# An adaptive-layer-norm block with holographic attention and a mixture of experts: adding DMAs for low weight halves, a sum moved into the inverse transform, and an epsilon moved to ScalarE

## The chip, the cores and the metric

The kernel runs on one core of a Trainium2 chip. The metric is the device time of one execution in microseconds (us); lower is better.

## The reference, cut to what matters

x has 4x1024 tokens of 256 features. The weights, a bias for each projection and the modulation vectors come in as inputs.

```python
def unit_projection(x):
    f = fft(x); f = f / (abs(f) + 1e-8); return ifft(f).real
h = layernorm(x) * (1 + ca) + sa
query, keys, values = (unit_projection(h @ W.T + b) for W, b in ((Wq, bq), (Wk, bk), (Wv, bv)))
s = cumsum(ifft(fft(keys) * fft(values)).real, axis=1)          # binding, running sum over tokens
x = x + ga * ifft(fft(s) * conj(fft(query))).real               # unbinding
h = layernorm(x) * (1 + cb) + sb
weights, sel = top_k(h @ gate_w, 2); weights = softmax(weights)
x = x + gb * sum(weights[k] * expert(sel[k], h))                # 8 experts, 256 -> 2x512 (swiglu) -> 256
```

## The kernel before, in words

The kernel has three stages. The attention stage goes over NBLK = 8 blocks of 512 tokens, t = 0 to 7. The routing stage sorts the (token, expert) pairs into tiles. The expert stage runs 39 tiles of up to 256 rows through the two expert products on TensorE. Each engine has its own program, written out by hand in one fixed order, and waits on semaphores; there is no scheduler. Iteration t of an engine's loop works on block t and also on neighbours of it.

In the attention stage the blocks are spectra with frequencies on the 128 partitions and tokens along the row. TensorE transposes the normalised rows (`project`, line 501), ScalarE scales them out of PSUM (`spectra`, line 894), and TensorE forms the six spectra (real and imaginary part of key, value, query) of block t+1 in `transform`, line 530. ScalarE copies these (line 909) and squares them (line 916) in `evacuate`. VectorE adds the squares (`magnitudes`, line 1305), ScalarE takes the roots (`roots`, line 935), and VectorE's `bind` adds epsilon to the value magnitudes (line 1248), multiplies the magnitudes, takes one reciprocal (line 1258), scales the spectra, multiplies key and value (line 1273) and runs the two running sums (lines 1282 and 1285). GpSimd multiplies the sums by the query's four combinations (line 1660; in block 7 VectorE takes half of them, line 1294), and in even blocks scales the inverse matrix (line 1669). VectorE's `unbind` adds two products to the real part (line 1299) and subtracts two for the imaginary part (line 1300). TensorE copies the Nyquist row (line 609), ScalarE writes it into the imaginary part (line 1033), and TensorE's `inverse` makes the rows of the block by two products for each of four token groups (lines 625 and 629). In block 7 it adds x by a third product with the identity (line 621).

The residual of a block is copied by ScalarE (`residual`, line 955), which stands inside `evacuate` two blocks on, behind the squares of the key. GpSimd then adds x to it by an accumulating DMA (line 1655). SP stores the sum (line 398), and VectorE takes its moments (line 1222, with the same line for the moments of a later block of x) behind the running sums of the next block. Then come `top2` on the gate scores of an earlier block, the Nyquist product (line 1241), `unbind`, `magnitudes` of the next block and the second layer norm (lines 1397 and 1402). ScalarE copies that to a high fp16 half (`split_rows`, line 966) and GpSimd forms the low half (`low_rows`, line 1646); SP stores both (line 422).

Beside this the expert weights are split into a high and a low fp16 half. They come in 24 chunks of 128x1024 fp32 numbers through a pair of staging buffers; SP loads chunk n (line 368) when the low half of chunk n-2 is out. ScalarE makes the high half by a scaled copy (`split_weights`, line 974), two chunks at the end of each iteration, behind `split_rows` and ahead of the next `evacuate`. The low half of the chunks 0 to 17 is made by TensorE in four pieces an iteration (`low_piece`, lines 589 and 590: 64 times the chunk less the high half, into a rotating PSUM bank), which ScalarE copies to fp16 (line 981). `psum_plan` gives the order in which four PSUM banks rotate among spectra, Nyquist columns, pieces, gate scores and Nyquist rows. ScalarE's standard deviations (lines 872 and 930) stand ahead of the pieces 1 and 2 and of line 1033; line 880 (four normalised row groups) follows line 1033, and then piece 3, the roots and the spectra.

Of the kernel before, what the change touches and what calls it, by code (L numbers as in the profile page):

```python
# [27 lines left out]
P = 128  # L28
# [6 lines left out]
BLK = 512  # L35
# [46 lines left out]
def psum_plan():  # L82

    items = []
    for t in range(-1, NBLK + 2):
        if t + 1 < NBLK:
            items += [("z", t + 1, i) for i in range(6)]
        if t == -1:
            items += [("ny", 0, 0), ("lo", 0, 0)]
        elif t == 0:  # L90
            items += [("pre", 0, 0), ("ny", 1, 0), ("row", 0, 0), *(("lo", 1, i) for i in range(4))]
            continue
        elif t < NBLK:
# [9 lines left out]
        if t < NBLK:  # L103
            items.append(("lo", t + 1, 2))
        if 0 <= t < NBLK:
            items.append(("row", t, 0))
        if t < NBLK:
            items.append(("lo", t + 1, 3))
    return {item: n for n, item in enumerate(items)}, items


def adaln_moe_kernel(nc, x, wqkv, bqkv, gate_w, w1, b1, w2, b2, c_t, wmod, dft, idft, ident, tri, iota, ramp, out):
# [11 lines left out]
    with ExitStack() as ctx:  # L124
# [73 lines left out]
        eps_col = carve(1)  # L198

# [115 lines left out]
        w_in = sems("w_in", 4)  # L315
        iota_in, gb_in = sem("iota_in"), sem("gb_in")
        w_lo = sems("w_lo", 2)
        lo_mm, w_hi, gate_split, h2_hi, h2_lo, hid_hi, y_mid = (sem(n) for n in (
# [39 lines left out]
        def load_weights(sp, n):  # L358

            if n in (18, 19):  # L360
                sp.wait_ge(prod_ready, 2 * NBLK)
            elif n >= 20:
                sp.wait_ge(w_lo[n % 2], 2 * (n // 2 - 1))
            elif n >= 2:
                sp.wait_ge(w_lo[n % 2], 2 * (n // 2))
            at = (n if n < W1_CHUNKS else W2_ORDER[n - W1_CHUNKS]) * WCH
            src = (w1 if n < W1_CHUNKS else w2)[:, at:at + WCH]
            sp.dma_start(staged(n), src).then_inc(w_in[stage_of(n)], 16)

# [79 lines left out]
        def _(pe):  # L449
# [162 lines left out]
            def inverse(t):  # L612
# [5 lines left out]
                for j in range(TPB):  # L618
                    cols = ps[:, OUT + j // 2, (j % 2) * D:(j % 2 + 1) * D]
                    if t == LAST:  # L620
                        pe.matmul(cols, ident_sb[:], x_sb[:, t % XS, j, :], start=True, stop=False)
                    if j == 0:
                        pe.wait_ge(g_ready, 2 * t + 1)
                        pe.wait_ge(ga_ready, t // 2 + 1)
                    pe.matmul(cols, prod[:, 0, RE, j * P:(j + 1) * P], idft_ga[:, RE, :], start=(t < LAST), stop=False)  # L625
                    if j == 0:
                        pe.wait_ge(g_ready, 2 * t + 2)
                        pe.wait_ge(row_ready, t + 1)
                    mm = pe.matmul(cols, prod[:, 0, IM, j * P:(j + 1) * P], idft_ga[:, IM, :], start=False, stop=True)  # L629
                    if t == LAST and j == 1:  # L630
                        mm.then_inc(l_idft, 1)
# [62 lines left out]
            for t in range(-1, NBLK):  # L694
# [20 lines left out]
                elif t + 1 < NBLK:  # L715
                    project(t + 1)
                    transform(t + 1)
                    low_piece(t + 1, 0)
# [5 lines left out]
                low_piece(t + 1, 1)  # L724
# [4 lines left out]
                low_piece(t + 1, 2)  # L729
                if t >= 0:  # L730
                    nyquist_row(t)
                low_piece(t + 1, 3)
# [104 lines left out]
        def _(act):  # L837
# [60 lines left out]
            def evacuate(t):  # L898
# [7 lines left out]
                for c in range(3):  # L906
# [6 lines left out]
                    if c == 2 and t >= 2:  # L913
                        low_piece(t, 0)
# [17 lines left out]
            def roots(t):  # L932
                act.wait_ge(mag_ready, t + 1)
                act.wait_ge(ny_out, 2 * t + 2)
                nc.scalar.activation(mag[:, t % 2], mag[:, t % 2], ACT.Sqrt).then_inc(root_ready, 1)

# [31 lines left out]
            def split_weights(n):  # L968
# [5 lines left out]
                nc.scalar.activation(parts_of(n)[HI], staged(n), ACT.Copy, scale=SW).then_inc(w_hi, 1)  # L974

            def low_piece(t, i):
# [3 lines left out]
                act.wait_ge(lo_mm, 4 * t + i + 1)  # L980
# [3 lines left out]
            def low_weights(t):  # L984

                act.wait_ge(g_ready, 2 * NBLK)
                for i in range(4):
                    act.wait_ge(lo_mm, 4 * t + i + 1)
# [40 lines left out]
            def nyquist_row(t):  # L1029

                act.wait_ge(row_mm, t + 1)
                act.wait_ge(g_ready, 2 * (t + 1))
# [15 lines left out]
            for t in range(-1, NBLK):  # L1048
# [32 lines left out]
                low_piece(t + 1, 1)  # L1081
                if t >= 2:
                    gate(t - 2)
                low_piece(t + 1, 2)
# [4 lines left out]
                low_piece(t + 1, 3)  # L1089
# [85 lines left out]
        def _(dve):  # L1175
            V = nc.vector
            V.memset(warm, 0.0).then_inc(warm_set, 1)
            V.memset(eps_col, EPS_LN)
            V.memset(ny_run[:, 0:1], 0.0)
# [109 lines left out]
            def unbind(t):  # L1289
# [9 lines left out]
                V.tensor_tensor(prod[:, 0, RE, 0:BLK], prod[:, 0, RE, 0:BLK], prod[:, 1, IM, 0:BLK], ALU.add).then_inc(g_ready, 1)  # L1299
# [342 lines left out]
        def _(pool):  # L1642
# [131 lines left out]
```

## Time and profile before

| | us |
|---|---|
| median of 3 runs | 595.83 |
| lowest and highest of them | 595.48, 599.93 |
| the profiled execution | 594.5 |
| its span in the profile | 592.5 |
| TensorE busy | 548.7 |
| VectorE busy | 478.2 |
| ScalarE busy | 294.4 |
| GpSimd busy | 294.8 |

The profile is of one execution. Its span runs from the first to the last recorded instruction; the execution's own time has 2 us around that. PE is TensorE's products, PEld its weight loads, DVE is VectorE, ACT ScalarE, POOL GpSimd, SPq the DMA issues of SP. A busy time is summed over the engine's instructions. An fp32 product shows as two instructions.

### The profile page before, as it was taken

Reading aid. Unit: us, or ns where it says so; the run is one execution under the profiler, and the core shown is the slowest. Engines: PE = TensorE matmul, PEld = TensorE weight load, DVE = VectorE, ACT = ScalarE, POOL = GpSimd, SP = SyncE. Lnnn points to the kernel's source line nnn. Section 1 sums busy time; section 2 is a strip of 40 time slices with the busy share of each in tenths; the row PEclk is TensorE's granted clock in tenths of the full one; section 3 lists DMA queues with packets and bytes.
Section 4 is the critical chain, followed back from the end, with each engine's and each line's share of the span. In section 5 each row is a group of like instructions: output and inputs, shape, how many; then the busy total and the mean of one; then the engine's idle time right before and its main releaser. Section 6 shows DMA issues by size and latency. Waiting matters only on the chain.

```text
span 592.5 us, 13011 instructions
## 1 busy us (share of the span) xinstructions
PE 548.7 (93%) x3955; PEld 407.6 (69%) x3956; DVE 478.2 (81%) x1059; ACT 294.4 (50%) x497; POOL 294.8 (50%) x197
## 2 busy tenths in 40 slices
PE   8998999999999995667999999999999999999992
PEld 6545565555646552526588888888888888888771
DVE  1288979999999989999488888888888888888762
ACT  4776678879696863641533333333333333333330
POOL 0004033432423242000548888888888888887532
PEclk9998989999897977866999999999999999999998
DMA  8333633653745437723567787777777777765722
GB/s 310 121 99 122 184 97 109 191 160 107 212 107 153 125 97 246 289 42 70 144 118 137 143 134 136 131 138 129 139 134 135 141 129 133 130 98 86 113 38 28
DMA packets 81571, 79.32 MB, mean 134 GB/s; under 512 B 44596, under 2 KB 71348, under 8 KB 81272
## 3 DMA queue, kind: packets, MB, share of 16 engines
q0 software_dynamic: 16912, 31.74, 30.2%
q1 hardware_dynamic: 63320, 46.15, 27.5%
q10 hardware_dynamic: 1296, 0.87, 0.5%
q8 instruction: 25, 0.41, 0.3%
q14 instruction: 18, 0.15, 0.1%
HBM read 44.06 MB, written 22.23 MB: 112 GB/s over the span
## 4 chain that ended last, share of the span: by engine, by line
PE 73%; DVE 17%; ACT 3%; issue 3%; DMA 2%; POOL 1%; POOLq 0%; DVEq 0%; ACTq 0%
PE ps L778 31%; PE ps L799 15%; PE ps L530 11%; PE ps L589 4%; DVE region L1258 2%; PE ps L543 2%; PE ps L629 2%; PE ps L625 1%; DMA region<-in_dft 1%; PE ps L600 1%; PE ps L461 1%; PE ps L590 1%; DVE region L1273 1%; DVE region L1380 1%; DMA out_rows<-w_stage,region 1%
## 5 line engine op out<-in xcount | busy, mean ns | idle before, releaser
L778 PE MATMUL ps<-region,w_sb 128*128 128x256 f16 (+1 forms) x1872 | 200.4, 264 | 1.9 <-ACT region L1026 1.3
L778 PEld LDWEIGHTS ps<-region,w_sb 128*128 x1872 | 172.6, 98 | 24.9 <-issue 3.2
L1690 POOL DMA_INDIRECT out_rows<-w_stage,region x71 | 135.7, 1912 | 49.6 <-issue 20.0
L1680 POOL DMA_INDIRECT region<-h_scratch,region x71 | 95.9, 1351 | 71.5 <-DVE region L1539 45.0
L1571 DVE TENSOR_SCALAR region<-ps,region 128x256 f32<-128x256 f32 (+1 forms) x156 | 64.3, 454 | 55.3 <-PE ps L778 53.8
L799 PE MATMUL ps<-region 128*128 x852 | 99.5, 273 | 3.5 <-DVE region L1585 3.3
L1130 ACT ACTIVATE region<-ps,region 128x256 f32<-128x256 f32 (+1 forms) x156 | 62.2, 451 | 79.2 <-PE ps L778 74.2
L1142 ACT ACTIVATE region<-region 128x1024 f16<-128x1024 f32 (+1 forms) x39 | 38.2, 981 | 109.4 <-DVE region L1579 106.8
L799 PEld LDWEIGHTS ps<-region 128*128 128x128 f16 x852 | 82.6, 98 | 14.4 <-issue 4.3
L530 PE MATMUL ps<-region 128*128 128x512 f32 x192 | 84.2, 595 | 3.2 <-ACT region L894 3.2
L1660 POOL TENSOR_TENSOR region<-region 128x512 f32<-128x512 f32 x30 | 37.3, 1270 | 96.2 <-DVE region L1285 96.2
L530 PEld LDWEIGHTS ps<-region 128*128 128x128 f32 x192 | 35.9, 190 | 46.9 <-issue 44.7
L589 PE MATMUL ps<-w_stage,ident_sw 128*128 128x512 f32 x72 | 47.0, 740 | 1.2 <-ACT region L974 1.2
L1579 DVE SCALAR_TENSOR_TENSOR region<-region 128x1024 f32<-128x1024 f32 (+1 forms) x39 | 44.0, 1129 | 1.4
L1585 DVE SCALAR_TENSOR_TENSOR region<-region 128x1024 f16<-128x1024 f32 (+1 forms) x39 | 43.8, 1124 | 1.1 <-ACT region L1142 1.1
L1646 POOL TENSOR_TENSOR region<-region 128x1024 f16<-128x1024 f32 x6 | 12.8, 2133 | 52.9 <-ACT region L966 45.4
L909 ACT ACTIVATE region<-ps,region 128x512 f32<-128x512 f32 x48 | 31.8, 683 | 11.1 <-PE ps L530 10.8
L1604 DVE SCALAR_TENSOR_TENSOR w_stage<-w_stage,region 128x256 f32<-128x256 f32 x71 | 31.3, 478 | 0.8
L1598 DVE SCALAR_TENSOR_TENSOR w_stage<-ps,region 128x256 f32<-128x256 f32 x71 | 26.8, 415 | 2.5 <-PE ps L799 2.4
L1258 DVE RECIPROCAL region<-region 128x516 f32<-128x516 f32 x8 | 27.0, 3378 | 0.3
L981 ACT ACTIVATE w_sb<-ps 128x512 f16<-128x512 f32 x32 | 18.7, 589 | 14.6 <-PE ps L590 14.4
L916 ACT ACTIVATE region<-region 128x1024 f32<-128x1024 f32 x24 | 25.3, 1055 | 0.5
(229 smaller groups left out, 699.2 us busy)
## 6 DMA issues: line engine op xcount, KB each, us to landing
w_stage<-in_w SPq DMA_DIRECT2D x20, 512.0 KB, 3.8
region<-in_x SPq DMA_DIRECT2D x8, 512.0 KB, 7.5
out_rows<-region SPq DMA_DIRECT2D x8, 512.0 KB, 3.0
h_scratch<-gb_bc SPq DMA_DIRECT2D x4, 1024.0 KB, 6.7
h_scratch<-region SPq DMA_DIRECT2D x8, 512.0 KB, 3.2
region<-region POOLq DMA_DIRECT2D x7, 512.0 KB, 4.6
region<-in_ramp SPq DMA_DIRECT2D x1, 2064.0 KB, 10.6
region<-in_w SPq DMA_DIRECT2D x4, 512.0 KB, 6.0
```

Source lines behind the costliest of these rows:

```text
L530: mm = pe.matmul(rot(("z", t, i)), w_spec[:, c, k, r * P:(r + 1) * P], h_t[:, k, :], start=(k == 0), stop=(k == KD - 1))
L589: pe.matmul(rot(("lo", t, i)), ident_sw[:], staged(n)[:, at:at + BLK], start=True, stop=False)
L778: mm = pe.matmul(ps[:, GV + 2 * half + a, (f % 2) * MT:(f % 2) * MT + wide], w, xg_t[:, s, xa * KD + k, 0:wide], start=(n == 0), stop=(n = ...
L799: mm = pe.matmul(ps[:, YB + s, u * D:(u + 1) * D], hid[:, s, xa, k, u * P:(u + 1) * P], w, start=(n == 0), stop=(n == 3 * KF - 1))
L1130: ins = nc.scalar.activation(gs[:, 2 * half + f, 0:wide], ps[:, 4 + 2 * half, f * MT:f * MT + wide], ACT.Gelu_apprx_sigmoid, scale=1.0 / S ...
L1142: nc.scalar.activation(hid[:, s, HI, :, 0:wide], vv[:, s, :, 0:wide], ACT.Copy, scale=SH / SUP).then_inc(hid_hi, 1)
L1258: V.reciprocal(rec, rec).then_inc(rec_ready, 1)
L1571: ins = V.tensor_scalar(vv[:, s, 2 * half + f, 0:wide], ps[:, 5 + 2 * half, f * MT:f * MT + wide], b1_t[:, bass.ds(e, 1), 1, 2 * half + f] ...
L1579: V.scalar_tensor_tensor(out=vv[:, s, :, 0:wide], in0=vv[:, s, :, 0:wide], scalar=(1.0 - LIMIT) * SUP, in1=gs[:, :, 0:wide], op0=ALU.max, ...
L1585: V.scalar_tensor_tensor(out=hid[:, s, LO, :, 0:wide], in0=vv[:, s, :, 0:wide], scalar=SH / SUP, in1=hid[:, s, HI, :, 0:wide], op0=ALU.mul ...
L1680: G.indirect_dma_start(out=xg_rows[:, t % XG, u, :], out_offset=None, in_=h_scratch, in_offset=bass.IndirectOffsetOnAxis(ap=gather_idx[:, ...
L1690: G.indirect_dma_start(out=out, out_offset=bass.IndirectOffsetOnAxis(ap=scatter_idx[:, at:at + 1], axis=0), in_=y_sb[:, t % 2, u, :], in_o ...
```

## The change

Chunks 4 to 15 no longer pass through TensorE. Behind the high half ScalarE overwrites the staging buffer with the high half times -1/64. GpSimd then loads the same chunk again from memory with an adding DMA into the staging buffer, which leaves the remainder, and ScalarE copies that times 64 as the low half (`low_chunk`). The pieces of chunks 0 to 3, 16 and 17 stay. The real sum of the unbinding (line 1299) goes: TensorE adds a third product per token group in `inverse`, with the same matrix. The epsilon of the value magnitudes (line 1248) moves to ScalarE, behind the roots. The new semaphores are w_neg, w_acc and unit_set; g_ready counts one instead of two for each block.

```diff
@@ psum_plan @@
-        elif t < NBLK:
+        elif t == NBLK - 1:
             items.append(("lo", t + 1, 0))
-            if t + 1 < NBLK:
-                items.append(("ny", t + 1, 0))
-        if t < NBLK:
+        elif t + 1 < NBLK:
+            items.append(("ny", t + 1, 0))
+        if t == -1 or t == NBLK - 1:
             items.append(("lo", t + 1, 1))
...
+        def summed(n):
+            return 4 <= n < 2 * NBLK
...
@@ pe inverse @@
                     if j == 0:
-                        pe.wait_ge(g_ready, 2 * t + 1)
+                        pe.wait_ge(x1_ready, 2 * t + 1)
                         pe.wait_ge(ga_ready, t // 2 + 1)
                     pe.matmul(cols, prod[:, 0, RE, j * P:(j + 1) * P], idft_ga[:, RE, :], start=(t < LAST), stop=False)
+                    if j == 0 and t < LAST:
+                        pe.wait_ge(x1_ready, 2 * t + 2)
+                    if j == 0 and t == LAST:
+                        pe.wait_ge(x1_own, 1)
+                    pe.matmul(cols, prod[:, 1, IM, j * P:(j + 1) * P], idft_ga[:, RE, :], start=False, stop=False)
                     if j == 0:
-                        pe.wait_ge(g_ready, 2 * t + 2)
+                        pe.wait_ge(g_ready, t + 1)
                         pe.wait_ge(row_ready, t + 1)
@@ pe loop (the same for the pieces 0, 2 and 3) @@
-                low_piece(t + 1, 1)
+                if t in (-1, LAST):
+                    low_piece(t + 1, 1)
@@ act evacuate @@
-                    if c == 2 and t >= 2:
-                        low_piece(t, 0)
@@ act roots @@
                 nc.scalar.activation(mag[:, t % 2], mag[:, t % 2], ACT.Sqrt).then_inc(root_ready, 1)
+                act.wait_ge(root_ready, t + 1)
+                nc.scalar.activation(mag[:, t % 2, VAL, :], mag[:, t % 2, VAL, :], ACT.Identity,
+                                     bias=eps_unit).then_inc(eps_ready, 1)
@@ act split_weights @@
                 nc.scalar.activation(parts_of(n)[HI], staged(n), ACT.Copy, scale=SW).then_inc(w_hi, 1)
+                if summed(n):
+                    act.wait_ge(w_hi, n + 1)
+                    nc.scalar.activation(staged(n), parts_of(n)[HI], ACT.Copy, scale=-1.0 / SW).then_inc(w_neg, 1)
+
+            def low_chunk(n):
+                act.wait_ge(w_acc[n % 2], 16 * (n // 2 - 1))
+                nc.scalar.activation(parts_of(n)[LO], staged(n), ACT.Copy, scale=SW).then_inc(w_lo[n % 2], 2)
@@ act loop (the same for piece 2 and chunk 2 * t + 3, behind the gate; piece 3 has no such part) @@
-                low_piece(t + 1, 1)
+                if t in (-1, LAST):
+                    low_piece(t + 1, 1)
+                else:
+                    low_chunk(2 * t + 2)
@@ dve bind, unbind @@
-                dve.wait_ge(root_ready, t + 1)
-                V.tensor_scalar(mag[:, s, VAL, :], mag[:, s, VAL, :], EPS_UNIT, None, ALU.add).then_inc(eps_ready, 1)
                 dve.wait_ge(eps_ready, t + 1)
...
-                V.tensor_tensor(prod[:, 0, RE, 0:BLK], prod[:, 0, RE, 0:BLK], prod[:, 1, IM, 0:BLK], ALU.add).then_inc(g_ready, 1)
@@ gpsimd @@
+            def add_weights(n):
+                pool.wait_ge(w_neg, n - 3)
+                G.dma_start(staged(n), source_of(n), accum_op=ALU.add).then_inc(w_acc[n % 2], 16)
+
             for t in range(NBLK):
                 s, b = t % 2, t // 2
                 if t >= 2:
                     pool.wait_ge(all_ready, t + 1)
                     low_rows(t - 2)
+                    for n in (2 * t + 2, 2 * t + 3):
+                        if summed(n):
+                            add_weights(n)
                 if t >= 1:
                     pool.wait_ge(x2_ready, t)
                     G.dma_start(x2, x_sb[:, (t - 1) % XS], accum_op=ALU.add).then_inc(x2_sum, 16)
+                if t == 1:
+                    for n in (4, 5):
+                        add_weights(n)
```

## Rows read from the trace of the kernel before

**Rows 1.** The page: busy time of each engine
```profile
PE 548.7 (93%) x3955; PEld 407.6 (69%) x3956; DVE 478.2 (81%) x1059; ACT 294.4 (50%) x497; POOL 294.8 (50%) x197
```

**Rows 2.** Chain of waits, core 0: start us, us, what
```profile
88.42 0.79 ACT region L894
...
138.86 0.45 PE ps L501 x4
...
139.34 0.79 ACT region L894
...
160.34 0.86 PE ps L589 x2
...
161.20 0.22 PE ps L590
...
164.59 0.43 PE ps L629 x2
...
165.50 0.79 ACT region L894
...
192.93 0.79 ACT region L894
...
218.94 0.71 DVE region L1250
```

**Rows 3.** Timeline of ScalarE: start us, us, line, idle before and who ended it
```profile
69.69 1.06 ACT L974 ACTIVATE w_sb<-w_stage 128x1024 f16<-128x1024 f32 x1 [3.43 <-DMA w_stage<-in_w]
...
141.63 1.99 ACT L974 ACTIVATE w_sb<-w_stage 128x1024 f16<-128x1024 f32 x2
...
143.52 1.25 ACT L909 ACTIVATE region<-ps,region 128x512 f32<-128x512 f32 x2
...
145.77 1.01 ACT L955 ACTIVATE region<-ps 128x1024 f32<-128x1024 f32 x1
...
157.28 0.28 ACT L930 ACTIVATE region<-region 128x4 f32<-128x4 f32 x1
...
161.03 0.59 ACT L1033 ACTIVATE region<-ps 1x512 f32<-1x512 f32 x1 [0.50 <-DVE region L1300]
...
163.97 1.48 ACT L935 ACTIVATE region<-region 128x1548 f32<-128x1548 f32 x1
```

**Rows 4.** Timeline of VectorE in block 4
```profile
139.59 0.42 DVE L1248 TENSOR_SCALAR region<-region 128x516 f32<-128x516 f32 x1
...
153.54 1.38 DVE L1222 BATCH_NORM_STATS2 region<-region 128x6 f32<-128x256 f32 x4
...
158.78 1.11 DVE L1299 TENSOR_TENSOR region<-region 128x512 f32<-128x512 f32 x1
...
159.81 1.13 DVE L1300 TENSOR_TENSOR region<-region 128x512 f32<-128x512 f32 x1
...
165.76 0.42 DVE L1248 TENSOR_SCALAR region<-region 128x516 f32<-128x516 f32 x1
```

**Rows 5.** Timeline of GpSimd in block 4
```profile
141.87 2.13 POOL L1646 TENSOR_TENSOR region<-region 128x1024 f16<-128x1024 f32 x1 [8.43 <-ACT region L966]
...
147.07 0.89 POOL L1655 DMA_DIRECT2D region<-region  x1 [3.07 <-ACT region L955]
```

**Rows 6.** Timeline of SP's queue in block 4
```profile
151.60 0.39 SPq L398 DMA_DIRECT2D out_rows<-region  x1
```

**Rows 7.** Stretches of DMA work: us, engines' busy us, clock, DMA share, GB/s
```profile
148.30:151.10 2.80, 2.80 (x8) 1.17 (x7) 2.77 (x3) 1.77 (x3) 0.00 (x0) 1.00 0.98 187
```

**Rows 8.** DMA issues of the page: KB each, median us from issue to landing
```profile
w_stage<-in_w SPq DMA_DIRECT2D x20, 512.0 KB, 3.8
...
region<-region POOLq DMA_DIRECT2D x7, 512.0 KB, 4.6
```

**Rows 9.** Stretches of TensorE: length, busy us (instructions), granted clock, DMA share, GB/s
```profile
183.00:184.00 1.00, 1.00 (x23) 0.50 0.37 122
...
189.00:190.00 1.00, 1.00 (x6) 1.00 0.00 0
```

More of the change, by code:

```diff
@@ L102, in psum_plan @@
             items.append(("gate", t - 2, 0))
-        if t < NBLK:
+        if t == -1 or t == NBLK - 1:
             items.append(("lo", t + 1, 2))
@@ L106, in psum_plan @@
             items.append(("row", t, 0))
-        if t < NBLK:
+        if t == -1 or t == NBLK - 1:
             items.append(("lo", t + 1, 3))
@@ L198, in adaln_moe_kernel @@
         eps_col = carve(1)
+        eps_unit = carve(1)
         wmod_sb = z_flat[:, 6 * NB:6 * NB + 6 * BLK].rearrange("p (k n) -> p k n", k=KD)
@@ L315, in adaln_moe_kernel @@
         w_in = sems("w_in", 4)
+        unit_set = sem("unit_set")
         iota_in, gb_in = sem("iota_in"), sem("gb_in")
         w_lo = sems("w_lo", 2)
+        w_neg, w_acc = sem("w_neg"), sems("w_acc", 2)
         lo_mm, w_hi, gate_split, h2_hi, h2_lo, hid_hi, y_mid = (sem(n) for n in (
@@ L368, in load_weights, with pieces_to, source_of @@
             sp.dma_start(staged(n), src).then_inc(w_in[stage_of(n)], 16)
+        def summed(n):
+            return 4 <= n < 2 * NBLK
+        def pieces_to(t, i):
+            return 4 * (t if t < 2 else t - NBLK + 2) + i + 1
+        def source_of(n):
+            at = (n if n < W1_CHUNKS else W2_ORDER[n - W1_CHUNKS]) * WCH
+            return (w1 if n < W1_CHUNKS else w2)[:, at:at + WCH]
         def parts_of(n):
@@ L717, in _ @@
                     transform(t + 1)
-                    low_piece(t + 1, 0)
                     nyquist_cols(t + 1)
@@ L728, in _ @@
                     gate(t - 2)
-                low_piece(t + 1, 2)
+                if t in (-1, LAST):
+                    low_piece(t + 1, 2)
                 if t >= 0:
                     nyquist_row(t)
-                low_piece(t + 1, 3)
+                if t in (-1, LAST):
+                    low_piece(t + 1, 3)
                 if t >= 0:
@@ L934, in roots @@
                 act.wait_ge(ny_out, 2 * t + 2)
+                if t == 0:
+                    act.wait_ge(unit_set, 1)
                 nc.scalar.activation(mag[:, t % 2], mag[:, t % 2], ACT.Sqrt).then_inc(root_ready, 1)
+                act.wait_ge(root_ready, t + 1)
+                nc.scalar.activation(mag[:, t % 2, VAL, :], mag[:, t % 2, VAL, :], ACT.Identity,
+                                     bias=eps_unit).then_inc(eps_ready, 1)
             def gate_rows(t):
@@ L979, in low_piece @@
                     act.wait_ge(tp_done, KD * NBLK)
-                act.wait_ge(lo_mm, 4 * t + i + 1)
+                act.wait_ge(lo_mm, pieces_to(t, i))
                 nc.scalar.activation(parts_of(2 * t + i // 2)[LO][:, (i % 2) * BLK:(i % 2 + 1) * BLK],
@@ L984, in low_weights @@
             def low_weights(t):
-                act.wait_ge(g_ready, 2 * NBLK)
+                act.wait_ge(idft_done, NBLK)
                 for i in range(4):
-                    act.wait_ge(lo_mm, 4 * t + i + 1)
+                    act.wait_ge(lo_mm, pieces_to(t, i))
                     nc.scalar.activation(parts_of(2 * t + i // 2)[LO][:, (i % 2) * BLK:(i % 2 + 1) * BLK],
@@ L1031, in nyquist_row @@
                 act.wait_ge(row_mm, t + 1)
-                act.wait_ge(g_ready, 2 * (t + 1))
+                act.wait_ge(g_ready, t + 1)
                 nc.scalar.activation(prod[0:1, 0, IM, 0:BLK], rot(("row", t, 0))[0:1, :], ACT.Copy).then_inc(row_ready, 1)
@@ L1080, in _ @@
                     std2(t - 1)
-                low_piece(t + 1, 1)
+                if t in (-1, LAST):
+                    low_piece(t + 1, 1)
+                else:
+                    low_chunk(2 * t + 2)
                 if t >= 2:
                     gate(t - 2)
-                low_piece(t + 1, 2)
+                if t in (-1, LAST):
+                    low_piece(t + 1, 2)
+                else:
+                    low_chunk(2 * t + 3)
                 if t >= 1:
@@ L1088, in _ @@
                     normal_rows(t + 2)
-                low_piece(t + 1, 3)
+                if t in (-1, LAST):
+                    low_piece(t + 1, 3)
                 if 1 <= t < NBLK - 1:
@@ L1178, in _ @@
             V.memset(eps_col, EPS_LN)
+            V.memset(eps_unit, EPS_UNIT).then_inc(unit_set, 1)
             V.memset(ny_run[:, 0:1], 0.0)
```

## The prediction

> **What bounds the kernel now.** I read the page's busy shares first: TensorE is busy 93% of the span, VectorE 81%, ScalarE and GpSimd 50% [rows 1]. A share does not say what a change in the attention part is worth, so the chain of waits came next. Up to 250 us it passes through one hand-over per block: the transposes of line 501 release ScalarE's spectra (line 894), and those release the transforms. Call the start of line 894 X. X was at 88.42, 139.34, 165.50 and 192.93 us [rows 2]: two blocks (t=2 and 3) took 50.92 us, t=4 26.16, t=5 27.43. After 290 us the expert part runs on TensorE alone, and nothing of the change reaches it.
>
> Block 4 in the timelines shows two full engines. VectorE goes from line 1248 at 139.59 to the next one at 165.76, 26.17 us, with no gap above 0.2 us [rows 4]. TensorE's transposes end where line 894 starts [rows 2]. Work taken off one of them alone would give nothing. This change takes work off both and gives it to ScalarE, GpSimd and the DMA queue, so the question is what these now hold up.
>
> **The parts, in block 4.** I count from X and from g, the end of line 1300 (159.81+1.13 = 160.94 [rows 4]).
>
> VectorE loses line 1248 (0.46 with its hand-over) and line 1299 (159.81-158.78 = 1.03; 0.6 in odd blocks, where GpSimd does not work beside it) [rows 4]. On its own it would need 24.7 us for block 4; without GpSimd beside it 24.4, which I take as its bound.
>
> TensorE loses four low pieces in each of t=1 to 6: 0.86+0.22 = 1.08 each [rows 2], 4.3 a block. It gains four products in the inverse transform, each a pair of instructions of 0.43 together [rows 2], 1.7 a block. Some 22.5 us are left, so its sum no longer binds. But the pieces stood ahead of g and most new products stand behind it. From g to the next X it was 165.50-160.94 = 4.56, with seven products behind the Nyquist row. Now ten are behind it; two of the twelve can run once GpSimd's products are there and g isn't. So g to X becomes 4.56+3x0.43 = 5.86.
>
> ScalarE loses four copies of line 981 a block, and gains two negatives, two low copies (both like line 974, 0.95 each back to back) and the epsilon (at most like line 909, 0.65). The low copies stand between line 930 (ends 157.56) and line 1033 (161.03) [rows 3], where ScalarE had only two low pieces: 157.5+2x0.95+0.15 = 159.55, against g at about 159.9. They cost nothing with top2 ahead of g (t=3 to 6), 0.5 us without (t=2); if that cover goes, they cost up to their 1.9. The epsilon ends at g+0.1+0.5+2.0+1.48+0.7 = g+4.8 (line 1033, four rows of line 880, roots), and VectorE comes for it at 165.76-160.94 = g+4.82: nothing, with no cover left, and up to 0.65 a block if it is late.
>
> The negatives are dear. Line 974 took 143.52-141.63 = 1.89 for two [rows 3]. A negative waits for its own high half, so the four take 2x(1.09+0.95) = 4.08: 2.2 more (bounds 1.9 if they pipeline, 2.4 if all drain). Line 955, the copy of the residual, stands behind them. It ended at 146.78, X+7.4; it will end at X+9.6.
>
> GpSimd waits for line 955 and adds x by an accumulating transfer (issued 147.07 [rows 5]); SP sees it landed at 151.60 [rows 6], 4.85 behind line 955. VectorE wanted it at 153.54, for line 1222 [rows 4]: 1.9 us of cover. Now it comes at X+9.6+4.85 = X+14.45. VectorE would be at line 1222 13.5 us after line 1250, which is at g+4.86 with X at g+5.86, so at X+12.5. The cover is gone and 1.95 us of wait take its place.
>
> The loop that sets the period then is: X to the sum 14.45; the sum to g, 5.24 for lines 1222 to 1299 and 0.7 for line 1300, or 1.05 beside GpSimd's line 1669 in even blocks, so 5.95 or 6.3; g to X 5.86. That is 26.25 or 26.6 us. Before, the same loop was 12.3+7.4+4.56 = 24.2 and lay under VectorE's 26.2.
>
> **The queue.** The adding loads go on GpSimd's DMA queue ahead of the x sum. Let δ be the delay they bring. The x transfer of 512 KB kept the 16 DMA engines busy from 148.30 to 151.10, share 0.98 [rows 7]; I take 2.7 us for an add too, the nearest row. The first can be issued when line 1646 ends, X+4.7 [rows 5], and move from X+6.0; the second moves to 11.4, where the x sum would begin at 11.2: δ 0.2. SP's store of h2 falls in the same stretch and can push all by 1.15: δ 1.35. I take 0.75, midway. Bounds: 0 if an add moves fast; 3.5 if each of the three holds the queue for 3.8, the time in which a plain load lands [rows 8].
>
> The Trainium skill ("DMA: Bandwidth & Descriptors", Anatomy of one DMA, SWDGE path) gives 2.0 us plus bytes over 436 GB/s, an estimate from that page of 3.2 us for 512 KB with 1.2 of moving. The trace disagrees for an accumulating transfer: 4.6 to landing, 2.8 of moving at 187 GB/s [rows 7, 8]. By the page δ would be 0 and the sum 3.8 us lower.
>
> **The clock.** TensorE's granted clock was 0.50 (1.2 GHz) at 183 us, after the light work of lines 543 and 564 and gaps between it, and 1.00 (2.4 GHz) again at 189 after further low pieces had run [rows 9]. The low pieces took the slow time on them and the inverse always ran fast. Without them TensorE has only light work from about X+12 to X+19.7, so I expect the inverse to start at the low clock and be the work that brings it back. If it stays low for R from the time that GpSimd's products are there, the 5.65 us of inverse and first transposes end R/2 later than 5.75, against 6.6 at full clock. R near 4 (the low stretches with low pieces in them lasted from under 4 to about 7 us) gives 1.15, R 2 nothing, R 7 gives 2.65. I take 1.0 for each X of t=1 to 5, 5 us; bounds 0 and 13. Blocks 0 and 7 keep their low pieces, and in t=6 no spectra follow.
>
> **The sum.** Blocks 0 and 1: VectorE's parts fall, but chunk 5 came only at 69.69 [rows 3], its negative delays the copies behind it, and the low copies push line 1033 by 1.5: the X at 88.42 comes 0.6 earlier. t=2 and 3: 2x26.2 against 50.92, +1.5. t=4: 26.6 against 26.16, +0.4. t=5: 26.2 against 27.43, whose pieces ran slowly, -1.2. t=6, to line 1250 at 218.94 [rows 2]: 14.45+6.3+4.85 = 25.6 against 26.0, -0.4. t=7: four more products, 1.7, partly beside ScalarE's lines 966 and 974, less line 1299: +0.7. Together +0.4, with 5δ = 3.75 and the clock's 5: +9.2. The profiled execution took 594.5 us (span 592.5), so 603.7. It lay 1.3 below the median of the runs, so I give 605 for that.
>
> **Rivals.** (1) VectorE stays the bound; faster. For it: it is the fullest engine and over 1 us leaves each block. It decides if the x sum lands over 1.95+δ earlier than worked out, and TensorE follows. Then t=3 to 6 take 24.4 each where they took about 105.1 together: -7.5; t=2 -1.5, blocks 0 and 1 -1: 584.5, on the median 586. Against it: the negatives stand ahead of line 955 in program order, and the cover was only 1.9. Chance 0.13. (2) The loop binds, but nothing queues and the clock is back in time: +0.4, 595, on the median 596; with one of the two at half price up to 600. For it: neither is seen in the trace before. Chance 0.34. (3) The adds are slow: the GpSimd queue decides from δ 2 on. At δ 3.5, 5x3.5 for 3.75 is +13.8 on my sum: 619. Against: the transfer like it took 2.8. Chance 0.08. My forecast, loop and queue and clock: 0.45, own range 600 to 612.
>
> 1% (6 us) is what a measurement tells from no change. Faster by more: 0.13 from (1). Same: 0.35, from (2) and the lower edge of mine. Slower: 0.52. The range 590 to 613 leaves out most of (1) and of (3).
>
> **What would show it.** VectorE waits 2 to 4 us at the first line 1222 behind the scans in t=2 to 6, released by the accumulating transfer. Line 955 starts some 8.6 us behind the first line 894, not 6.4. Two adds stand between lines 1646 and 1655. From g to the next X 5.9 to 7.5 us, with the first products of the inverse at granted clock 0.50. Blocks of 27 to 29 us. If VectorE doesn't wait, (1) holds and the forecast is wrong; if inverse products start at 1.00, the clock's term is; if the wait is over 5 us, it is (3).

## The result, and the profile after

The kernel after took 615.07 us (median of 3 runs, 612.92 to 616.55) where the kernel before took 595.83. The ratio is 1.029, 95% interval 1.024 to 1.034: slower. The sign and the main cause were as forecast; 615 lies above the range (590 to 613), and 10 us above the 605. The two medians alone would give 1.032; the ratio is nearer to that of the means, and one of the three executions of the kernel before took 599.93. The profiled execution took 616.55 us with a span of 614.5, against 594.5 and 592.5.

The page's busy times and queues:

```profile
PE 546.8 (89%) x3947; PEld 417.1 (68%) x3948; DVE 472.9 (77%) x1044; ACT 309.2 (50%) x505; POOL 303.9 (49%) x209
...
PE 65%; DVE 14%; DMA 10%; ACT 5%; issue 4%; POOL 1%; POOLq 0%; SPq 0%; DVEq 0%; ACTq 0%
...
w_stage<-in_w POOLq DMA_DIRECT2D x12, 512.0 KB, 7.6
...
region<-region POOLq DMA_DIRECT2D x7, 512.0 KB, 6.9
```

Both full engines of before are a little less busy than in [rows 1] and yet the span is 22 us longer, so the loss is not work added to them. DMA is now 10% of the chain that ended last, 2% before. An adding load takes 7.6 us from issue to landing (median), and the x sum 6.9, 4.6 before [rows 8].

The chain of waits up to the start of block 4's loop (start us, us, what; line 517 is line 501 of before, 546 is 530, 917 is 894, 932 is 909, 981 is 955, 1264 is 1222; 641, 646 and 650 are the three inverse products, the second of them new; 1003 is the negative copy, 1008 the low copy, 1283 is 1241, 1290 is 1250, 1339 is 1300, 625 is 609 and 1067 is 1033):

```profile
92.61 0.79 ACT region L917
...
121.76 0.79 ACT region L917
...
143.78 1.01 PE ps L625 x4
144.79 0.85 PE ps L641 x2
...
148.21 0.60 PE ps L646 x2
148.81 0.43 PE ps L650 x2
...
151.84 0.45 PE ps L517 x4
152.31 0.79 ACT region L917
```

Against [rows 2] the spectra of block 2 begin 4.2 us late (92.61 for 88.42) and the hand-over then takes 29 to 31 us a block, not 25 to 27. The rest of block 4 is in the timelines of ScalarE, GpSimd, SP and VectorE (start us, us, line; in brackets the idle time before and who ended it):

```profile
158.68 1.25 ACT L932 ACTIVATE region<-ps,region 128x512 f32<-128x512 f32 x2
...
160.92 1.01 ACT L981 ACTIVATE region<-ps 128x1024 f32<-128x1024 f32 x1
...
154.85 2.56 POOL L1685 TENSOR_TENSOR region<-region 128x1024 f16<-128x1024 f32 x1 [14.56 <-ACT region L992]
...
157.36 0.86 POOL L1690 DMA_DIRECT2D w_stage<-in_w  x1
159.07 0.86 POOL L1690 DMA_DIRECT2D w_stage<-in_w  x1 [0.86 <-ACT w_stage L1003]
162.22 0.86 POOL L1702 DMA_DIRECT2D region<-region  x1 [2.29 <-ACT region L981]
...
169.16 0.39 SPq L414 DMA_DIRECT2D out_rows<-region  x1
...
155.45 2.51 DVE L1303 TENSOR_TENSOR region<-region 128x516 f32<-128x516 f32 x1
...
169.17 1.41 DVE L1264 BATCH_NORM_STATS2 region<-region 128x6 f32<-128x256 f32 x4 [3.93 <-DMA region<-region]
...
173.54 0.14 DVE L1283 TENSOR_TENSOR region<-ps,region 128x4 f32<-128x4 f32 x1
...
173.89 0.69 DVE L1339 TENSOR_TENSOR region<-region 128x512 f32<-128x512 f32 x1
...
179.80 0.70 DVE L1290 SCALAR_TENSOR_TENSOR region<-region 128x516 f32<-128x516 f32 x1 [0.32 <-ACT region L960]
```

VectorE had no gap above 0.2 us in [rows 4]; now it waits 3.93 us for the x sum. That is the transfer whose cover the prediction saw vanish. Over the five blocks with adds (t=2 to 6) these waits are 3.9, 4.1, 3.9, 4.3 and 5.0.

The inverse transform of that block, in TensorE's timeline, and the stretches of its light work and its products (length, busy us and instructions of the five engines, granted clock, DMA share, GB/s):

```profile
173.74 1.01 PE L625 MATMUL ps<-ident_sb,region 128*1 128x128 f32 x4 [4.50 <-DVE region L1283]
174.55 1.06 PE L641 MATMUL ps<-region 128*128 128x256 f32 x2
...
178.81 0.76 PE L650 MATMUL ps<-region 128*128 128x256 f32 x2
179.41 0.59 PE L641 MATMUL ps<-region 128*128 128x256 f32 x2
```
```profile
158.50:169.00 10.50, 9.31 (x72) 6.05 (x71) 6.67 (x7) 9.82 (x15) 5.34 (x5) 1.00 0.97 196
174.50:178.00 3.50, 3.50 (x11) 2.75 (x10) 3.50 (x8) 3.50 (x7) 0.00 (x0) 0.50 1.03 312
```

TensorE stands idle for 4.50 us until VectorE's line 1283 and then runs its first five products at a granted clock of 0.50 (1.2 GHz): 0.85 from one pair to the next, 0.43 behind. Before, the pairs of this transform took 0.43 [rows 2]. The clock had fallen at 168.95, behind light work (lines 559 to 592) and 0.3 us before this idle time began, and it was back at about 179.15. The DMA engines are busy for 0.97 of 10.5 us while two adds, the x sum and SP's store pass.

Block 4's loop against the prediction's terms (X the start of line 917, g the end of line 1339):

| step | predicted | measured |
|---|---|---|
| X to the end of line 981 | 9.6 | 161.93-152.31 = 9.62 |
| to line 1264, the x sum landed | 4.85+0.75 = 5.6 | 169.17-161.93 = 7.24 |
| to g | 6.3 | 174.58-169.17 = 5.41 |
| g to the next X | 5.86+1.0 = 6.86 | 182.65-174.58 = 8.07 |
| whole | 28.35 | 30.34 |

### The profile page after: what moved, and what is told of

The parts are those of the page before. It is cut to its first block, busy times and chain, and to the rows that moved or that the text cites. A ratio compares the mean times of both kernels' runs of the same rounds, so it can differ in the third digit from the quotient of the medians.

```text
span 614.5 us, 12988 instructions
## 1 busy us (share of the span) xinstructions
PE 546.8 (89%) x3947; PEld 417.1 (68%) x3948; DVE 472.9 (77%) x1044; ACT 309.2 (50%) x505; POOL 303.9 (49%) x209
## 4 chain that ended last, share of the span: by engine, by line
PE 65%; DVE 14%; DMA 10%; ACT 5%; issue 4%; POOL 1%; POOLq 0%; SPq 0%; DVEq 0%; ACTq 0%
PE ps L801 30%; PE ps L822 14%; DMA region<-region 7%; PE ps L546 6%; DMA w_stage<-in_w 3%; PE ps L650 2%; PE ps L641 2%; PE ps L646 2%; DVE region L1264 2%; PE ps L469 1%; ACT region L932 1%; DVE region L1298 1%; PE ps L616 1%; PE ps L477 1%; ACT region L981 1%
## 5 line engine op out<-in xcount | busy, mean ns | idle before, releaser
L1264 DVE BATCH_NORM_STATS2 region<-region 128x6 f32<-128x256 f32 x60 | 20.8, 411 | 22.6 <-DMA region<-region 21.1
L932 ACT ACTIVATE region<-ps,region 128x512 f32<-128x512 f32 x48 | 30.6, 679 | 5.6 <-PE ps L546 5.6
L625 PE MATMUL ps<-ident_sb,region 128*1 128x128 f32 x32 | 7.7, 389 | 22.9 <-DVE region L1283 22.9
```

The source lines that it names most:

```text
L932: nc.scalar.activation(z[:, t % 2, c, r, 0:BLK], rot(("z", t, 2 * c + r)), ACT.Identity, bias=bias_f[:, 3 * r + c:3 * r + c + 1]).then_inc ...
```

## The experiments

Ratios are to the kernel before, timed again beside each group of runs (medians 594.2, 594.8 and 594.3), with 95% intervals. Medians of one kernel scatter by 2 to 3 us, so intervals between hand-overs (X to X) are compared beside them. The 1.029 of the change rests on three executions on either side, so half a percent between it and a run below is not resolved. "Waits" are VectorE's for the x sum in t=2 to 6.

**The pieces back on TensorE; the moved sum and epsilon stay.** From the kernel before:

```diff
-V.tensor_tensor(prod[:, 0, RE, 0:BLK], prod[:, 0, RE, 0:BLK], prod[:, 1, IM, 0:BLK], ALU.add)
+pe.matmul(cols, prod[:, 1, IM, j * P:(j + 1) * P], idft_ga[:, RE, :], start=False, stop=False)
-V.tensor_scalar(mag[:, s, VAL, :], mag[:, s, VAL, :], EPS_UNIT, None, ALU.add)
+nc.scalar.activation(mag[:, t % 2, VAL, :], mag[:, t % 2, VAL, :], ACT.Identity, bias=eps_unit)
```

> The adding loads, the negatives and the low copies are undone: TensorE makes all low halves by pieces as before; the sum in the inverse and the epsilon on ScalarE stay. Theory (loop: the negatives and adds delay the x sum, and the inverse runs at the low clock for want of pieces ahead of it): the wait of VectorE for the x sum goes to 0, the inverse runs at granted clock 1.00, but TensorE, full before, has 1.7 us more a block: 603 to 607 us. Rival A (the third product alone is the loss, whatever stands ahead of it): about the time of the changed kernel, 612 to 616. Rival B (all of the loss is the adds): 594 to 597.

600.98 us, 1.0105 (1.0067 to 1.0143). No waits, intervals 24.6 to 29.1, inverse pairs at 0.43. That is less than the 603 to 607 expected. Undoing the adding loads and what serves them takes away 1.85% (1.0292/1.0105), nearly two thirds of the loss, and leaves about 1%. The parts need not add up so in another order, as the next run shows.

**The real sum back on VectorE, in the kernel after.**

```diff
+V.tensor_tensor(prod[:, 0, RE, 0:BLK], prod[:, 0, RE, 0:BLK], prod[:, 1, IM, 0:BLK], ALU.add)
-pe.matmul(cols, prod[:, 1, IM, j * P:(j + 1) * P], idft_ga[:, RE, :], start=False, stop=False)
```

> Only the sum of the real part goes back to VectorE (eight products a block in the inverse); adds and epsilon stay as changed. Theory: the wait for the x sum stays at 4 to 5 us a block, g comes 0.7 later and the inverse saves four products at a clock that is low for half of them, 1.7 to 2.5 us: 608 to 612 us. Rival A (the third product is the loss): 596 to 600. Rival B (all of the loss is the adds): 613 to 617.

612.28 us, 1.0290 (1.0243 to 1.0338): the ratio shows no difference from the change. The waits stay at 4.0 to 5.1. The profiled execution shows a small one: intervals of 28.6 to 29.8 in t=2 to 5 in place of 29.1 to 30.6, and g to X of 5.1 to 6.4 us in place of 7.7 to 8.2, of which the later g takes back more than half. So while the x sum binds, returning the sum is worth under 1 us a block of 30, and the medians do not tell it from nothing.

**The x sum ahead of the two adds in GpSimd's queue.**

```diff
-low_rows(t - 2); add_weights(2 * t + 2); add_weights(2 * t + 3); G.dma_start(x2, ...)
+low_rows(t - 2); G.dma_start(x2, ...); add_weights(2 * t + 2); add_weights(2 * t + 3)
```

> The changed kernel with GpSimd's x sum issued ahead of the two adding loads of the block. Theory (the x sum queues behind the adds, 7.2 us from line 981 to landing where it was 4.85): it lands 4.9 us after line 981 again, VectorE's wait falls by 2.4 in t=2 to 6, up to 12 us; the low copies come to wait for the later adds and give back about 1 us a block: 603 to 609 us. Rival C (the x sum is late only because ScalarE's negatives stand ahead of it, the queue has no part): the landing stays near 7 us behind line 981 and the time at 613 to 616.

611.66 us, 1.0282 (1.0232 to 1.0333), where 603 to 609 was expected. The x sum landed 5.2 us behind the copy, not 7.2, and the waits fell to 1.6 to 3.1. Yet intervals stayed near 30.6: the adds came later, and ScalarE's low copy, line 1008, stands ahead of the row copy of line 1067 that the inverse needs. ScalarE's timeline:

```profile
170.27 1.04 ACT L1008 ACTIVATE w_sb<-w_stage 128x1024 f16<-128x1024 f32 x1
...
172.76 1.06 ACT L1008 ACTIVATE w_sb<-w_stage 128x1024 f16<-128x1024 f32 x1 [1.36 <-DMA w_stage<-in_w]
173.72 0.57 ACT L1067 ACTIVATE region<-ps 1x512 f32<-1x512 f32 x1
```

So the queue does delay the x sum, but the order only chooses which of three transfers is late.

**Twelve idle products on TensorE ahead of line 625, t=1 to 6.** They add work that nothing uses.

```diff
+for _ in range(12):
+    pe.matmul(rot(("row", t, 0)), ident_h[:], w1_sb[:, HI, 0:BLK], start=True, stop=True)
 nyquist_row(t)
```

> The changed kernel with twelve idle fp16 products of 512 columns into the bank of the Nyquist row, in t=1 to 6, ahead of the row's transposes. They compute nothing that is used. Theory (the inverse starts at the low clock because only light work stands ahead): the inverse's products run at 1.00, 0.43 a pair, g to the next X falls from 8.1 to about 5.4 us, five times: 600 to 604 us. Rival D (the slow pairs are slow for another reason, such as operands or a busy memory port): pairs stay at 0.85 and the time at 613 to 617.

611.48 us, 1.0274 (1.0231 to 1.0316). Its chain of waits:

```profile
166.32 5.14 PE ps L755 x12
171.46 0.44 PE ps L625 x4
171.90 0.43 PE ps L641 x2
172.33 0.43 PE ps L646 x2
```

All pairs but one run in 0.43, and g to X falls from 8.07 to 6.26 us. The granted clock was 0.50 in 166 to 170, under the idle products, and 1.00 from 172: they took the slow time on them. So the slow pairs come from the want of such products ahead of the inverse, and not from its operands or the DMA beside it. The 600 to 604 expected was missed: the span is 7.5 us shorter, but the ratio gains only 0.2%. The profiled executions exaggerate, since 616.55 was the highest of the change's three and 608.83 the lowest of this kernel's four; the ratio may hide some, since all four (up to 612.3) lie below all three of the change (from 612.92). What the mechanism is worth in the whole stays between the two.

**Epsilon back on VectorE, in the kernel after.**

```diff
-nc.scalar.activation(mag[:, t % 2, VAL, :], mag[:, t % 2, VAL, :], ACT.Identity, bias=eps_unit)
+V.tensor_scalar(mag[:, s, VAL, :], mag[:, s, VAL, :], EPS_UNIT, None, ALU.add)
```

> Only the epsilon goes back to VectorE. Theory: VectorE comes 0.3 us early for it in the changed kernel but waits 4 us for the x sum later in the same block, so the move costs and saves nothing while the loop binds: 611 to 615 us, X to X the same within 0.3 us. Rival: the epsilon behind the roots delays bind and with it the loop by 0.3 to 0.7 a block: 608 to 611.

617.43 us, 1.0367 (1.0330 to 1.0404), above the 611 to 615 expected. Nothing comes back. The intervals of t=2 to 5 are the change's within 0.35 us (29.5, 30.6, 30.2, 30.4), as expected; the profiled execution is 2.2 us longer because the spectra of block 2 begin at 94.72 and not at 92.61. That start is unsteady: the run with the x sum first and the one with late copies, whose programs are the same up to there, have 90.59 and 94.78. So the extra is not shown to be epsilon's. The 0.32 us for which VectorE waits at line 1290 is not a loss.

**Eight of the twelve products ahead of line 625.** Those that need no g, in a loop of their own.

```diff
+if t >= 1:
+    inverse_head(t)    # RE and the third product, all four j; t=1 to 7
 nyquist_row(t)
 if t in (-1, LAST):
     low_piece(t + 1, 3)
```

> The changed kernel with the eight products of the real part (two a token group) issued ahead of the Nyquist row's transposes in t=1 to 7; the four imaginary products stay behind. Same products, other order. Theory (the new products cost because program order puts them between g and the next X, at the low clock, while TensorE idles some 4 us ahead): g to the next X falls from 8.1 to 4 to 5 us, in five blocks 15 to 20 us: 594 to 600 us. Rival (the loop passes over the x sum and the adds alone, and X would be held by something else): under 5 us gained, 608 to 612.

615.88 us, 1.0347 (1.0303 to 1.0390), far above both the 594 to 600 expected and the rival's 608 to 612. Odd blocks fell to 25.2, 27.7 and 27.6, even ones took 30.8 and 30.6. In even blocks GpSimd scales the inverse matrix behind its products, and TensorE's program order then holds up the row transposes:

```profile
168.84 1.20 POOL region L1755 x2
...
170.18 3.62 PE ps L638 x8
173.80 1.73 PE ps L650 x8
175.53 0.45 PE ps L625 x4
...
176.00 0.02 ACT region L1103
```

The row copy (line 1103 there) came at 176.00, 3.6 behind g, and with it the roots and epsilon, for which VectorE then waited 3.47 us. The first four of the eight products ran at a granted clock of 0.50, 0.9 us each for 0.43, so the low clock makes about half of the 3.6. An early start is worth 2 to 3 us where the matrix is ready, and where it isn't it gains nothing or costs up to 1.7 (30.8 for 29.15 in t=2). By the X of block 6 this run was 5.0 us ahead (208.24 for 213.26) and it lost them again from there on: block 7 has the same order, with x's four products besides.

**The x sum first, and the high and negative copies of chunks 6 to 15 behind the residual copy.** The order of GpSimd's queue is that of the third run; ScalarE's calls at the end of each iteration go for these chunks.

```diff
 residual(t - 2)
+split_weights(2 * t)
+split_weights(2 * t + 1)
```

> The changed kernel with the x sum issued ahead of the adds, and with ScalarE's high halves and negatives of the chunks 6 to 15 moved behind the residual's copy (line 981). Theory: line 981 ends at X+7.0 rather than 9.6 minus nothing else, actually about X+5.6 as the high halves go too; the x sum lands at X+11; VectorE's wait goes to 0 to 0.5; but ScalarE's four copies now stand ahead of the standard deviations and low copies, so some 2 us come back: dX 27 to 28 where it was 30.4, 600 to 605 us. Rival (the adds' own landing holds the low copies and so line 1067, whatever the order): dX stays above 29.5, 609 to 614.

603.18 us, 1.0122 (1.0083 to 1.0162): the largest step of all. ScalarE's and VectorE's timelines:

```profile
147.66 1.45 ACT L917 ACTIVATE region<-ps,region 128x512 f32<-128x512 f32 x2 [1.89 <-PE ps L517]
...
153.97 1.01 ACT L983 ACTIVATE region<-ps 128x1024 f32<-128x1024 f32 x1
154.88 1.05 ACT L1002 ACTIVATE w_sb<-w_stage 128x1024 f16<-128x1024 f32 x1
...
160.79 1.38 DVE L1266 BATCH_NORM_STATS2 region<-region 128x6 f32<-128x256 f32 x4
```

The residual copy (line 983) ends 7.3 us behind X, as before the change, and VectorE finds the sum there: one wait of 0.24 us in t=2, none behind it. Intervals are 26.2 to 28.2. Against the run with the queue order alone (1.0282) only the copies moved, so these four copies ahead of the residual were 1.6% of the time, nearly 10 us. The loop theory holds. Late copies with the old queue order were not run.

**The same, with the first of the three products ahead of line 625.**

> e7's order together with the four first products (prod 0 RE) ahead of the Nyquist row's transposes, the four third products right behind them, then the four imaginary ones. Theory: both halves of the loop shrink, dX 25 to 26.5 (then ScalarE or VectorE with 24.4 binds): 586 to 594 us, at or below the kernel before. Rival (TensorE's low clock at these products keeps them slow): dX 27 to 28, 597 to 603.

611.63 us, 1.0270 (1.0235 to 1.0306). It gives the gain back, where 586 to 594 was expected: even blocks take 29.8 and 29.9, the row copy comes 5.3 us behind g. The fault of the run with eight products, again: in block 4 GpSimd's scaling ends at 168.56, four products at the low clock take 3.75, and the transposes come behind them.

**Late copies and eight idle products.** The late-copy run with eight of the idle products ahead of line 625, t=1 to 6.

> The previous late-split kernel (the x sum ahead of the two weight adds, high and negative copies of chunks 6 to 15 behind the residual copy) plus 8 idle half-precision products on TensorE ahead of each nyquist row transpose in blocks 1 to 6, so that the inverse products find the clock at its full level. Theory (two separate costs in the loop, the DMA's late landing and the inverse transform at half clock): VectorE's waits for the x sum stay near 0, g to the next spectra falls from about 8.0 to 6.3 us, an interval from about 27 to about 25.5 us, ratio to before 1.000 to 1.007, 596 to 599 us. Rival (a third chain, GpSimd's or ScalarE's, is right behind): intervals stay at 26.5 or more and the ratio at 1.010 to 1.014.

607.07 us, 1.0207 (1.0160 to 1.0253), worse than without them, with intervals of 28.2 to 29.3 in t=2 to 5. Its TensorE timeline:

```profile
136.82 0.80 PE L592 MATMUL ps<-region 128*128 128x8 f16 x24 [1.70 <-ACT region L974]
137.48 3.38 PE L755 MATMUL ps<-w_sb,ident_h 128*128 128x512 f16 x8
140.70 0.60 PE L625 MATMUL ps<-ident_sb,region 128*1 128x128 f32 x4
```

VectorE had the input of line 625 ready at 136.72, and g came at 138.18; the idle products held the transposes until 140.70. Where the x sum was late they filled a wait, and where it is on time they are in the way. My expectation of 596 to 599 took their time as free; the rival's figure was nearer, for another reason.

**And chunks 4 and 5 in TensorE's pieces again.** The run ahead of this one, with the adding loads from chunk 6 on.

```diff
-return 4 <= n < 2 * NBLK
+return 6 <= n < 2 * NBLK
```

> As the run ahead of it, but the low halves of chunks 4 and 5, the first two that the change gave to the DMA, are made by TensorE's pieces as before, and the adding DMAs start at chunk 6. Theory (the loss in block 1 is chunk 5's add, which lands 10 us after its issue beside SP's stores and loads and holds ScalarE's row copy): the spectra of block 2 begin at 88.5 to 90.5 us and not at 94 to 95, and the end comes 3.5 to 5 us earlier than in the run ahead of it, 592 to 595 us, ratio 0.994 to 1.000. Rival (the start only looks late, since ScalarE's other work of block 1 is what bounds it): the spectra of block 2 begin within 1 us of the run ahead of it, same time.

610.63 us, 1.0269 (1.0221 to 1.0317). Missed: the spectra of block 2 came at 91.78, not at 88.5 to 90.5, and later than the 90.13 of the run ahead. The pieces and the eight idle products lie in a row on TensorE (4.3 and 1.7 us of its chain) and cost as much as chunk 5's landing did.

**Late copies, chunks 4 and 5 in pieces, real sum on VectorE, no idle products.**

> The late-split kernel with chunks 4 and 5 on TensorE's pieces and the real sum of the unbinding back on VectorE (8 inverse products a block and not 12), no idle products. If the eight products all stand behind g at half clock, g to the next spectra is 6.3 to 7 us, VectorE pays 0.3 to 0.7 us ahead of g in its place: intervals of 25.5 to 26.5 us, ratio 0.998 to 1.006, 594 to 599 us. If moving the sum to TensorE is worth what it was meant to be, the run is 1 to 3 us above the run ahead of it; if the sum on TensorE costs, it is below it.

597.49 us, 1.0029 (0.9995 to 1.0063): level with the kernel before. Spectra of block 2 at 89.83, intervals 25.1 to 28.5 in t=2 to 5. This is the best form of the adding loads found, and it isn't faster than before. It differs from the late-copy run (1.0122) by the 0.9% of the sum and the two chunks together.

**The real sum on TensorE alone, in the kernel before.** The first two lines of the first diff.

> The kernel before with one part of the change alone, the real sum of the unbinding done by TensorE in the inverse transform (12 products in place of 8, one VectorE add less); pieces and epsilon stay as before. An earlier run had the sum and epsilon together at 1.0105 of before. Theory (four more products behind g, at half clock where the clock is low there, about 1.7 us, less the 0.5 us of the add, over six blocks): 0.5 to 1.0 per cent slower, 598 to 601 us, g to the next spectra 1 to 2 us longer than before. Rival (epsilon on ScalarE is what cost): within 0.3 per cent of before.

600.42 us, 1.0099 (1.0072 to 1.0126). The sum alone costs 1%, and epsilon has nothing left to explain (1.0105 with it). TensorE's timeline (625, 630 and 634 are the three inverse products):

```profile
134.69 0.60 PE L609 MATMUL ps<-ident_sb,region 128*1 128x128 f32 x4
135.13 1.02 PE L589 MATMUL ps<-w_stage,ident_sw 128*128 128x512 f32 x2
...
136.21 0.59 PE L625 MATMUL ps<-region 128*128 128x256 f32 x2
...
140.96 0.60 PE L634 MATMUL ps<-region 128*128 128x256 f32 x2
```

Twelve pairs at full clock, and g (134.95) to X (142.03) takes 7.08, 4.57 before the change (134.77 to 139.34). The clock has no part in it: four more products at 0.43 are 1.7 us, on a TensorE that was already full, and none starts before the last low piece ends, 1.1 us behind g. The hand-over looks worse than it is: g came 19.26 us behind X where it had come 20.93, since VectorE lost its add, and TensorE did not follow. X to X went from 25.50 to 26.34, so the sum costs 0.84 us in this block.

## Why the prediction was right, and where it was wrong

By its own steps, in the profiled spans (22.0 us longer):

| part | predicted | measured |
|---|---|---|
| blocks 0 and 1, to the X at 88.42 | -0.6+1.0 | 92.61-88.42 = 4.2 |
| t=2 and 3 | 1.5+1.5+2.0 = 5.0 | 59.70-50.92 = 8.8 |
| t=4 | 2.15 | 30.34-26.16 = 4.2 |
| t=5 | 0.55 | 30.61-27.43 = 3.2 |
| t=6, to line 1290 | 0.35 | 25.68-26.01 = -0.3 |
| t=7 and on | 0.7 | 375.56-373.56 = 2.0 |
| sum | 9.2 | 22.1 |

The step that failed is the term δ of the queue: 0.75 us a block in the prediction, 2.0 to 3.0 measured, 2.6 in the mean. Over five blocks that is 9.2 of the 12.8 us by which the sum fell short, and 605 with it is 614. From g to X added 4.2 in t=2 to 5, block 1 3.8 and t=7 1.3, and the stretch from the sum to g gave back 6.3; the half microsecond left is rounding. The signs named ahead say the same: the waits (3.9 to 5.0) lie about or above the upper end of 2 to 4, g to X (7.7 to 8.2) above 5.9 to 7.5, and the intervals of t=2 to 5 (29.1 to 30.6) above 27 to 29.

**Right.** X to the end of line 981, 9.62 for 9.6: the four copies cost what a copy each in series costs. That the x sum becomes the bound: VectorE waits for it in every block with adds from t=2 on, and the late copies take the ratio from 1.028 to 1.012 and the waits away. Epsilon and, from t=2 on, the low copies at nothing: epsilon's return gave nothing, and ScalarE's line 1067 follows g by 0.5, ahead of the first product that needs it. Rival (1), VectorE as the bound, is refuted.

**δ, "I take 0.75, midway".** Mis-sized. In t=4 it was 7.24-4.85 = 2.4, and 2.0 to 3.0 in the others, between my value and the bound of 3.5. I took 2.7 us of moving for each transfer and the store of h2 at half its price. DMA queues of the stretch 158.5:169.0 (packets, MB, share of the 16 engines):

```profile
q0 software_dynamic: 432, 1.57, 82.3%
q1 hardware_dynamic: 487, 0.48, 15.2%
```

GpSimd's queue had 0.823x10.5 = 8.6 us for its three transfers, 2.9 each, and the other queue's 0.48 MB, SP's store issued at 157.43, took the other 1.6 in full. So the size was the upper one of the two that I had averaged, and more: 1.35 for the store's case, three times 0.2 for the slower transfers, and 0.45 because the store took 1.6 and not the 1.15 for which the prediction has no row. That makes 2.4, by working out; no run takes the store away. My rival (3) let the queue decide from δ 2 on, and δ was 2.0 or more in all five blocks, though no wait passed 5 us, its sign. At δ 3.5 it said 619, nearer to 615 than my 605, and it had a chance of 0.08: I had the mechanism and gave its size too little. The Trainium skill ("DMA: Bandwidth & Descriptors", Anatomy of one DMA, SWDGE path) gives an estimate of 3.2 us for one transfer of 512 KB, 1.2 of it moving; the trace disagrees again, with 2.9 of moving for each of three in a row, and the measurement decides.

**"Two of the twelve can run once GpSimd's products are there and g isn't."** Wrong. TensorE's program has line 625 ahead of the inverse, and line 625 waits for VectorE's line 1283, 0.9 us ahead of g. GpSimd's products were ready at 170.35 (its four products of line 1710 took 4.96 from 165.39), and TensorE idled to 173.74. In even blocks GpSimd's scaling of the matrix, to 171.54 here, would have held an early start too, a wait that I hadn't read. All twelve stand behind g. The sum alone, at full clock, made g to X 2.5 us longer where I had 1.3, of which 1.7 is g coming earlier. The run with eight products ahead shows the price of forcing the early start.

**The clock's 1.0.** Direction right, size too low. With all four added products behind g, g to X is 4.56+4x0.43 = 6.3 at full clock; the run with idle products has 6.26. It measured 8.07 with the first five pairs at 0.85, so the low clock costs 1.8. I let the slow work begin before g; it begins with the transposes, because nothing ran between 169.24 and them. In t=2, 3 and 5 g to X was 7.76, 7.69 and 8.17.

**Block 1.** Missed. I had it 0.6 earlier. The first two adds are issued beside SP's stores and loads, and the chain of waits has

```profile
73.76 10.38 DMA w_stage<-in_w
...
85.18 0.58 ACT region L1067
```

Chunk 5 lands at 84.14, 10.4 us after its issue, and its low copy, ahead of the row copy in ScalarE's order, moves that from 83.50 to 85.18. The other 2.5 us are the twelve products, five at the low clock. Its X at 65.53 was already 1.7 later than before (63.87), as it was without the adding loads (65.46). The start of block 2 is also unsteady from one execution to another, by up to 4 us in two runs with the same program up to there (90.59 and 94.78), so this row's 4.2 is of one execution. I had cost the low copies by ScalarE's time and not by the landing they wait for. The try to mend it with pieces was confounded by the idle products and leaves open how much the landing alone is worth.

**t=6 and the sum to g.** From the sum to g was 5.4, 0.9 shorter than my 6.3, and only 3.4 in t=6, where no next block's rows are normalised behind the wait; I had used the same 6.3. That error hid some of the others.

**Still open.** How much the idle products save in the whole, between 0.2% and the 7.5 us of the profiled spans; whether the late copies would do as much without the new queue order; and how the adds and the sum share what is left between 1.003 and 1.0.

## What to carry to other kernels

When two engines are both full, look for the hand-over with the least cover, here 1.9 us at the accumulating transfer, and ask what each moved instruction puts ahead of it in every queue it passes. Work for an idle engine goes behind the operation that feeds a critical transfer: with the queue order the same, that took the ratio from 1.028 to 1.012 here. Before counting work as "can run early", read the engine's program order for what stands in front of it.

## What was not expected of the hardware

- Three accumulating transfers of 512 KB in a queue landed 7.6 us (adds) and 6.9 us (x sum) after issue in the median, where one alone had 4.6. They share the engines: with the x sum first it landed in 4.9 and the adds in 8.9, and the time of the block hardly changed.
- A VectorE instruction of 128x516 in f32 with two tensor inputs (lines 1300 and 1303) takes 0.70 us, but took 2.33 to 2.57 in the five blocks t=2 to 6, each time the one that began while GpSimd's line 1685 ran (154.85 to 157.41 in block 4). It ended 0.55 to 0.56 us behind GpSimd's end in all five, as if it waited for that instruction to end; line 1300, begun 0.13 us ahead of it in block 4, kept its 0.70. Before the change GpSimd's instruction fell on the reciprocal of line 1258, which has one input and takes 3.38 us with or without it, and all eight of line 1263 took 0.70. The change only moved the phase; in this kernel the wait for the x sum hides the 1.6 to 1.9 us. The Trainium skill ("GPSIMD Engine Reference", Specifications) says that GpSimd's way to SBUF is shared with VectorE and that VectorE's instructions with two inputs from SBUF contend for it; the slowed instructions and the undisturbed reciprocal agree.
- Taking work off TensorE lowered its clock: the mean granted clock fell from 0.944 to 0.912. The pieces that were removed had stood ahead of the inverse products, which in blocks 1 to 6 took 0.43 a pair throughout. The mean says little about the time, though: the run of 597.49 us had 0.917, and the run of 600.42 had 0.950.
